# Masking the lower form of the relative scores on GpSimd in 28 of 64 heads

## The reference, cut to what matters

```python
term1 = einsum('bhqd,bhkd->bhqk', Q, K);  term2 = einsum('bhqd,kd->bhqk', Q, r)
term3 = einsum('hd,bhkd->bhk', u, K)[:, :, None, :]
term4 = einsum('hd,kd->hk', v, r)[None, :, None, :]
scores = (term1 + term3 + _rel_shift(term2 + term4)) / sqrt(dk)   # pad a column, reshape, cut
attn = softmax(scores, axis=-1)
out = einsum('bhqk,bhkd->bqhd', attn, V).reshape(B, S, H * dv)
```

## Time and profile before

| | |
|---|---|
| median of 3 runs | 2711.02 us |
| the profiled execution | 2714.78 us, span 2713.0 us |
| TensorE busy | 2590.3 us (95%), granted clock 0.986 of full |
| VectorE busy | 2045.4 us (75%) |
| ScalarE busy | 2094.2 us (77%) |
| GpSimd busy | 896.3 us (33%) |
| line 939, the mask matmuls | 576, 123.6 us with overlaps |
| line 1688, GpSimd's zeroing | 128, 635 ns each |

### The profile page before, as it was taken

The page is one execution under the profiler, slowest core; times in us unless marked ns, Lnnn a source line. Parts: engine busy times, 40 slices in busy tenths (PEclk is TensorE's granted clock), DMA queues, the critical chain, the costliest instruction groups (busy, mean ns, idle before and its releaser), DMA issues.

```text
span 2713.0 us, 107218 instructions
## 1 busy us (share of the span) xinstructions
PE 2590.3 (95%) x43752; PEld 1552.6 (57%) x43752; DVE 2045.4 (75%) x5518; ACT 2094.2 (77%) x3769; POOL 896.3 (33%) x1605
## 2 busy tenths in 40 slices
PE   5999999999999999999999999999999999999996
PEld 3566666555655556666666666666644444444444
DVE  6799898422222238889888888988889999999993
ACT  3787787899999986666667666666688888888884
POOL 2212323230312523612631461252134326333221
PEclk7999999999999999999999999999999999999997
DMA  3535343443424432312321241223122323223221
GB/s 113 147 99 161 97 125 104 127 122 96 122 82 126 135 116 79 115 51 60 111 84 52 83 119 52 83 68 90 42 66 80 97 71 98 67 65 110 68 74 33
DMA packets 197218, 250.16 MB, mean 92 GB/s; under 512 B 48292, under 2 KB 113124, under 8 KB 196728
## 3 DMA queue, kind: packets, MB, share of 16 engines
q1 hardware_dynamic: 193272, 240.54, 30.1%
q10 hardware_dynamic: 3456, 2.77, 0.4%
HBM read 132.89 MB, written 100.07 MB: 86 GB/s over the span
## 4 chain that ended last, share of the span: by engine, by line
PE 70%; DVE 22%; issue 4%; ACT 2%; DMA 1%; POOL 0%; ACTq 0%; SPq 0%; DVEq 0%; POOLq 0%
PE ppv L1073 27%; DVE mx L1404 16%; PE ring L936 8%; PE ring L981 7%; PE ring L921 5%; PE ring L947 4%; PE ring L1014 3%; PE ring L1115 2%; PE ring L1179 1%; PE ring L1100 1%; PE ring L988 1%; PE ring L1170 1%; PE ring L1122 1%; PE ring L1030 1%; PE ring L939 1%
## 5 line engine op out<-in xcount | busy, mean ns | idle before, releaser
L1236 ACT ACTIVATE probs<-ring 128x512 f32<-128x512 f32 (+1 forms) x3280 | 1969.2, 684 | 553.4 <-PE ring L936 283.7
L1404 DVE TENSOR_REDUCE mx<-ring 128x1 f32<-128x512 f32 (+2 forms) x2112 | 1276.3, 646 | 164.4 <-PE ring L981 77.6
L1073 PE MATMUL ppv<-probs,values 128*32 128x128 f32 x30208 | 1107.6, 278 | 5.0 <-ACT probs L1236 2.1
L1073 PEld LDWEIGHTS ppv<-probs,values 128*32 128x32 f32 x30208 | 752.4, 110 | 335.2 <-issue 162.2
L1399 DVE CUSTOM_DVE_ANT_0 seen<-ring,low_seen 128x512 f32<-128x512 f32 x576 | 392.0, 681 | 58.4 <-PE ring L981 58.4
L988 PE MATMUL ring<-kst,qst 48*128 48x512 bf16 (+1 forms) x1060 | 350.7, 388 | 28.1 <-DMA kst<-records_k 16.7
L947 PE MATMUL ring<-qst,kst 51*128 51x512 bf16 (+2 forms) x1092 | 343.8, 383 | 3.9 <-DMA qst<-mrow 1.6
L1658 POOL CAST mparts<-mall 128x8 bf16<-128x8 f32 x192 | 36.6, 191 | 760.6 <-DVE mall L1422 673.6
L1688 POOL TENSOR_SCALAR_AFFINE_SELECT probs<-probs 128x512 f32<-128x512 f32 x128 | 81.3, 635 | 541.5 <-ACT probs L1236 323.5
L981 PE MATMUL ring<-kst,qst 112*128 112x512 bf16 (+3 forms) x768 | 250.6, 327 | 1.2 <-DVE zsc L1541 0.8
L936 PE MATMUL ring<-qst,kst 115*128 115x512 bf16 (+3 forms) x768 | 250.9, 327 | 0.0
(11 more groups left out here) (154 smaller groups left out, 3000.2 us busy)
## 6 DMA issues: line engine op xcount, KB each, us to landing
qst<-records_q SPq DMA_DIRECT2D x448, 96.0 KB
heads_out<-osb SPq DMA_DIRECT2D x256, 128.0 KB, 2.0
kst<-records_k SPq DMA_DIRECT2D x320, 96.0 KB
records_k<-parts SPq DMA_DIRECT2D x90, 256.0 KB
records_q<-parts SPq DMA_DIRECT2D x90, 256.0 KB
kst<-records_k SPq DMA_DIRECT2D x128, 102.0 KB
oT<-heads_out SPq DMA_DIRECT2D x60, 128.0 KB, 2.8
proj<-proj SPq DMA_DIRECT2D x96, 64.0 KB, 2.0
```

Of the source, the lines that this page charges most:

```text
L1073: mm = pe.matmul(ppv[32 * g:32 * g + 32, c:c + P], values[:, (n // H) % 2, v:v + 32], src[:, at * P:(at + 1) * P], start=u == 0 and qt < 4 ...
L1236: nc.scalar.activation(probs_of(rd.n, u), src, ACT.Exp, scale=1.0 if rd.s == RBF else SCALE).then_inc(s_exp, 1)
L1404: ins = dve.tensor_reduce(mx[:, slot, to:to + 1], bank[:, at * P:(at + nt) * P], AX.X, ALU.max)
```

## The change

`BUSY` is the set of rounds in which the planner puts a GpSimd piece. `LOW_BY_POOL` holds the relative heads n for which neither round n nor round n + 1 is in it: 28 heads, 136 to 142, 152 to 158, 168 to 174 and 184 to 190. In these, `unit_kq` issues no mask matmul, and GpSimd sets the same elements of `probs` to zero after the exponential: `hide` does one `affine_select` on the diagonal tile of 128 x 128 (8 units) and a `memset` of one element (7 units), in GpSimd's stream one slot after the unit's. `take_values` waits for these in the nine units. The other 36 heads are as they were, and so are units 8 and 17 of all.

```diff
+BUSY = {max(m for m in range(LAST) if ROUNDS[m].tick <= AT[name]) for name in AT if name[0] == "pool" and 0 <= name[1] < INTERVALS}
+LOW_BY_POOL = {n for n in range(REL * HEADS, (REL + 1) * HEADS) if n not in BUSY and n + 1 not in BUSY}
+def hidden_in(n, unit):
+    kt, q0, _, _ = unit[0]
+    if upper(unit):
+        return 1
+    return (q0 <= kt < q0 + 4) + (q0 < kt <= q0 + 4) if n in LOW_BY_POOL else 0
+def hidden_to(n, u):
+    return sum(hidden_in(m, unit) for m in range(REL * HEADS, n) for unit in KQ_UNITS[REL]) + \
+        sum(hidden_in(n, unit) for unit in KQ_UNITS[REL][:u + 1])
...
-                        m0, m1 = max(first, lo), min((kt + 1) * P, hi)
+                        m0, m1 = (lo, lo) if n in LOW_BY_POOL else (max(first, lo), min((kt + 1) * P, hi))
...
-                if rd.s == REL and upper(rd.kq[u]):
-                    pe.wait_ge(s_up, 2 * (n - REL * HEADS) + (2 if final else 1))
+                if rd.s == REL and hidden_in(n, rd.kq[u]):
+                    pe.wait_ge(s_up, hidden_to(n, u))
...
-            def hide_upper(n, u):
+            def hide(n, u):
+                unit, tile = ROUNDS[n].kq[u], probs_of(n, u).rearrange("p (t q) -> p t q", t=4)
                 pool.wait_ge(s_exp, ROUNDS[n].exps + u + 1)
...
+                if upper(unit):
+                    pool.affine_select(tile, tile, [[0, 4], [-1, P]], ALU.is_ge, 0.0, base=-2, channel_multiplier=1).then_inc(s_up, 1)
+                    return
+                (kt, q0, _, _), = unit
+                if q0 <= kt < q0 + 4:
+                    own = tile[:, kt - q0]
+                    pool.affine_select(own, own, [[1, P]], ALU.is_ge, 0.0, base=0, channel_multiplier=-1).then_inc(s_up, 1)
+                if q0 < kt <= q0 + 4:
+                    pool.memset(tile[0:1, kt - q0 - 1, P - 1:P], 0.0).then_inc(s_up, 1)
...
-                        hide_upper(rd.n - 1, 17)
-                    if u == 9 and rd.n >= 0 and rd.s == REL:
-                        hide_upper(rd.n, 8)
+                        hide(rd.n - 1, 17)
+                    if u and rd.n >= 0 and rd.s == REL and hidden_in(rd.n, rd.kq[u - 1]):
+                        hide(rd.n, u - 1)
```

More of the change, by code:

```diff
@@ L1682, in next_values @@
                                    zexp[:, i % 2].unsqueeze(2).to_broadcast([P, NT, VCOLS]), ALU.mult).then_inc(s_zv, 1)
-            def hide_upper(n, u):
+            def hide(n, u):
+                unit, tile = ROUNDS[n].kq[u], probs_of(n, u).rearrange("p (t q) -> p t q", t=4)
                 pool.wait_ge(s_exp, ROUNDS[n].exps + u + 1)
-                tile = probs_of(n, u).rearrange("p (t q) -> p t q", t=4)
-                pool.affine_select(tile, tile, [[0, 4], [-1, P]], ALU.is_ge, 0.0, base=-2, channel_multiplier=1).then_inc(s_up, 1)
+                if upper(unit):
[7 more added lines that the diff above has]
+                    pool.memset(tile[0:1, kt - q0 - 1, P - 1:P], 0.0).then_inc(s_up, 1)
             def next_scores(n):
```

## The result

| | before | after |
|---|---|---|
| median | 2712.14 us (13 runs) | 2698.08 us (13 runs) |
| ratio, 95% interval | | 0.9947 [0.993, 0.9964] |
| profiled span | 2713.0 us | 2696.4 us |
| relative stage, 64 rounds (from slot 6 of round 127 to slot 6 of round 191) | 956.42 us | 942.65 us |

What follows compares the result with a forecast made beforehand. TensorE was taken to bound the 28 changed heads; 0.50 us of masks per head gave 14.0 us, GpSimd's work hidden: 2711.0 - 14.0 = 2697.0 us (-0.52%), range 2692 to 2706.

Steps and rivals of the forecast that it cites:

- The bound: The 28 changed heads: TensorE is busy throughout and bounds them; VectorE is next, 1.71 us away in a 13.76 us round.
- The price of a mask: TensorE's stream: 0.06 us per mask from start to start, 0.03 for a single column; 0.50 us per head taken.
- the sum: Whole kernel: 14.0 us off for 28 heads, from 2711.0 to 2697.0 us.
- GpSimd's price: GpSimd, per head: 8 affine_select at 0.25 us and 7 memset at 0.10, 2.7 us; at most 5.5.
- The cover: Unit 4's values: 0.95 us between exponential and TensorE, 0.61 needed for the zeroing chain, 0.34 us to spare.
- The transposed maxima: GpSimd in slot 1: unit 0's zeroing ends at 1181.0, before split_max's 1181.15; a slip of 0.2 us would cost nothing.
- The tightest place: Unit 2 of a head, behind the six-exponential burst: 0.20 us left after two masks go, holding by 0.02 us.
- rival (a): TensorE waits in score bursts or at unit 4: 5 us lost, 2702 us; both at once 2707; chance 0.14.
- (b): ScalarE's pace in all four bursts or a slow GpSimd chain eats all: 2711 us; chance 0.08 together with (d).
- (c): GpSimd and VectorE obstruct each other in SBUF: 28 us more, 2739 us; chance 0.06 with anything slower.
- (d): Rounds behind each stretch, waiting for DMAs, give the gain back: 2711 us; chance 0.08 together with (b).
- "faster": Whole kernel: chance 0.86 of a gain counting as a change, under 0.2% (5.4 us) being the same.

Runs made afterwards that it cites:

- e3: The kernel before, with each mask matmul of the 28 heads issued twice: median 2727.14 us, ratio 1.0061 to the kernel before.
- e1: The changed kernel without GpSimd's zeroing and the waits for it, masks still left out (wrong output): median 2698.09 us, ratio 0.9956 to the kernel before.
- e4: The changed kernel with unit 4's affine_select done three times, each waiting for the one before: median 2706.95 us, ratio 0.9981 to the kernel before.
- e2: The changed kernel with the mask matmuls kept beside GpSimd's zeroing: median 2711.08 us, ratio 0.999 to the kernel before.

## Why the prediction was right

**The bound.** TensorE without a gap, read from windows and chain: confirmed from both sides, by the change itself (fewer masks, 13.8 us less) and e3 (more masks, 12.9 us more). e1 adds that GpSimd's zeroing and TensorE's waits for it take nothing from the gain.

**The price of a mask.** 0.50 us per head from starts; the rounds went from 13.76 to 13.26. The stage gives 13.8 us where the sum had 14.0, between its two readings of the price (13.5 by the chain, 14.3 by the starts). The durations in the page (0.22 us each) would have given 28 x 9 x 0.22 = 55 us.

**GpSimd's price.** The quarter tile was put at 0.25 us between two bounds: it takes 0.24 from start to start (1183.27 to 1183.51), 0.29 by duration. The `memset` took 0.09 (0.10 taken). 2.5 us per round came, 2.7 were worked out.

**The cover.** 0.34 us of spare time at unit 4 was worked out, 0.42 is what e4 shows. Most of the difference is the way from GpSimd to TensorE: 0.09 + 0.10 for the weight load were taken, and in e4 the batch goes on 0.14 us after the `memset` (1181.02 to 1181.16). The transposed maxima: `split_max` starts 1.77 us into the round (1180.10 - 1178.33) instead of 1.70 (1181.15 - 1179.45), 0.07 later where none was expected; it costs nothing, as said.

**The tightest place.** Unit 2 starts at 1179.21 and the exponential it needs ends at 1177.43 + 2 x 0.49 + 0.60 = 1179.01: the 0.20 us worked out. The margin of 0.02 held. No matmul waited there; what grew in the round is a wait of weight loads beside running matmuls, from 0.2 to 0.4 us in all:

```profile
PEld ring L956 <- ACT probs L1256: 0.4, 2, 0.2
```

So rival (a) didn't come. (b) needs a chain longer than its cover, which e4 makes and which then costs 0.31 us per head. (c) fell with e2. (d) fell with the stage's time: the rounds behind each stretch are as long as before, to 0.02 us but for two that moved by 0.16 in opposite directions.

One figure of the prediction contradicts itself: "faster" was to hold all of rival (a), but both halves of (a) at once were priced at 2707 us, a gain of 4 us, under the 5.4 us that count as a change. It didn't come to bear.

What I judged less well is how far the choice could be widened. For all 64 heads I expected the change to end some 25 us behind itself and it ended 14.0 behind, with both of its terms off; for the choice by unit I expected 8 us more and got 6.4.

## What to carry to other kernels

Where TensorE is the bound, a matmul is worth the time from its start to the next start, and that only if nothing runs beside it in the other rows of the array: a mask of 128 columns was worth 0.06 us in one stage and had no time of its own in another. Work moved to an engine with idle time was free here as long as its result was there before the bound engine came; work out that spare time for the nearest consumer, then for the longest thing that can be queued ahead on the helping engine, and choose by piece of work rather than by round. When nearly all of a program's rounds repeat to about 0.01 us, as here, compare the rounds, not the spans.

## What the runs showed of the hardware

`affine_select` on GpSimd: 128x128 f32 takes 292 ns and 0.24 us from start to start, 128x512 635 ns and 0.60; a `memset` of one element 88 ns. A second mask matmul right behind the first, with the same weights loaded again, added 0.47 us per nine where the first nine were worth 0.50. VectorE's reductions out of PSUM kept their 682 to 683 ns while GpSimd's busy time beside them nearly doubled (18.32 to 35.44 us). The six exponentials in a row went on at 0.49 us each from start to start with 0.60 us duration, whether TensorE's scores came every 0.47 or every 0.44 us.
